# Attention and mixture-of-experts layer on one core: output weights pair by pair, logits in the attention's bank, router work half a step later

## What is computed

```python
# attention: 16 heads of size 64
n = layernorm(x)
q, k, v = (einsum('bsd,hde->bhse', n, W) for W in (Wq, Wk, Wv))
p = softmax(causal(q @ k.T / sqrt(64)))
y = n + concat_heads(p @ v) @ Wo
x = x + layernorm(gamma * norm(y, eps=1e-3) + beta)
# mixture of 8 experts, 2 for each token
t = layernorm(x)
probs = softmax(t @ router_w)              # the "logits" are t @ router_w
top_p, top_i = top_k(probs, 2)
out = sum over the 2 experts: top_p * (gelu(t @ w1[e]) @ w2[e])
x = x + layernorm(out)
```

## Time before and how to read the profile

| | us |
|---|---|
| median of 3 runs | 779.05 |
| lowest and highest | 778.43, 781.7 |
| profiled execution, its own time | 777.79 |
| its span, first to last instruction | 776.0 |
| PE busy | 720.2 (93%) |
| PE weight loads busy | 603.3 (78%) |
| DVE busy | 580.1 (75%) |
| ACT busy | 521.5 (67%) |
| POOL busy | 290.2 (37%) |

### The profile page before, as it was taken

How to read it: one execution, slowest core, us unless ns; L and a number is a source line. 1 busy time by engine, 2 the same in 40 slices (tenths; PEclk the granted TensorE clock), 3 DMA queues, 4 the chain that set the end, 5 groups by cost and what they waited for, 6 DMA issues and landing times.

```text
span 776.0 us, 17672 instructions
## 1 busy us (share of the span) xinstructions
PE 720.2 (93%) x5954; PEld 603.3 (78%) x5955; DVE 580.1 (75%) x1914; ACT 521.5 (67%) x1687; POOL 290.2 (37%) x404
## 2 busy tenths in 40 slices
PE   4999999999999999999999999999977789999954
PEld 3788878878788788878888888878767779999921
DVE  4668898989888888988889888988877444444316
ACT  4777777878777777877777777877754434444506
POOL 3024444232333423242333423241416555555525
PEclk9999999999999999999999999999979999999978
DMA  8620000000000000000000000000021132222145
GB/s 180 198 40 8 8 15 16 14 23 8 22 12 18 22 16 20 11 22 8 22 12 19 22 15 22 9 15 8 16 64 49 56 116 81 70 77 72 49 156 187
DMA packets 43701, 34.88 MB, mean 45 GB/s; under 512 B 10624, under 2 KB 40320, under 8 KB 43616
## 3 DMA queue, kind: packets, MB, share of 16 engines
q1 hardware_dynamic: 37984, 23.81, 11.4%
q0 software_dynamic: 4544, 9.45, 3.4%
q10 hardware_dynamic: 1088, 0.54, 0.2%
HBM read 20.22 MB, written 13.56 MB: 44 GB/s over the span
## 4 chain that ended last, share of the span: by engine, by line
PE 83%; DVE 4%; issue 4%; ACT 3%; POOL 2%; another core or an unknown queue 1%; DMA 1%; DVEq 1%; POOLq 0%; ACTq 0%; SPq 0%
PE PT1O L421 11%; PE M L383 9%; PE SC L404 8%; PE A L432 7%; PE A L664 7%; PE M L385 6%; PE M L384 6%; PE SC L412 4%; PE PT1O L441 4%; PE PT L446 3%; PE PT L445 3%; PE SC L407 3%; PE SC L383 2%; PE SC L385 2%; POOL expert_rows L1465 2%
## 5 line engine op out<-in xcount | busy, mean ns | idle before, releaser
L1201 ACT ACTIVATE qk<-M 128x512 f32<-128x512 f32 x127 | 76.0, 599 | 104.6 <-PE M L385 102.9
L1212 ACT ACTIVATE prob<-SC,nmax 128x256 f32<-128x256 f32 x256 | 125.4, 490 | 0.0
L1465 POOL DMA_INDIRECT expert_rows<-v_sb,got x78 | 77.4, 993 | 61.8 <-issue 31.1
L421 PE MATMUL PT1O<-pT,v_sb 128*64 128x256 f32 (+1 forms) x1024 | 98.6, 335 | 0.7 <-ACT pT L1217 0.7
L1206 ACT ACTIVATE prob<-SC,nmax 128x128 f32<-128x128 f32 x256 | 96.4, 377 | 4.3 <-DVE nmax L767 4.3
L421 PEld LDWEIGHTS PT1O<-pT,v_sb 128*64 128x64 f32 x1024 | 64.1, 138 | 42.7 <-ACT pT L1217 23.4
L775 DVE TENSOR_TENSOR prob<-prob,rden 128x512 f32<-128x512 f32 x128 | 92.5, 723 | 4.5 <-DVE rden L773 0.2
L1457 POOL DMA_INDIRECT sent_rows<-rec,slot x64 | 69.8, 1090 | 55.0 <-DVE slot L975 37.2
L767 DVE TENSOR_REDUCE nmax<-SC 128x2 f32<-128x512 f32 x128 | 87.1, 680 | 0.0
L383 PE MATMUL M<-xt_hi,wqk_hi 128*128 128x256 f32 x254 | 82.3, 324 | 4.4 <-ACT xt_st L1196 1.4
L664 PE MATMUL A<-w_sb,hidT 128*128 x624 | 78.0, 279 | 6.7 <-ACT v_sb L1335 3.3
(11 more groups left out here) (193 smaller groups left out, 1821.9 us busy)
## 6 DMA issues: line engine op xcount, KB each, us to landing
got<-sent_rows SPq DMA_DIRECT2D x39, 132.0 KB
w_in<-expert_rows SPq DMA_DIRECT2D x16, 256.0 KB, 3.5
x_in<-L_attn_x SPq DMA_DIRECT2D x16, 128.0 KB, 2.0
w_in<-L_ffn_w SPq DMA_DIRECT2D x1, 2048.0 KB, 12.1
x_res<-L_attn_x SPq DMA_DIRECT2D x16, 128.0 KB, 2.0
w_sb<-L_ffn_w SPq DMA_DIRECT2D x8, 256.0 KB, 4.7
out<-y_out SPq DMA_DIRECT2D x8, 256.0 KB, 2.1
sent_rows<-pad_rec SPq DMA_DIRECT2D x11, 132.0 KB, 4.8
```

What stands on the lines that cost most here:

```text
L421: last = mm(PT1O[k * E:(k + 1) * E, cols], v_sb[:, t, h * E:(h + 1) * E], src[:, par, k, :], start=(t == 0), stop=(t == 1), skip_group_che ...
L1212: return a.activation(prob[:, slot, k, 1:3, :].rearrange("p n t -> p (n t)"), SC[par][:, k, LATE_Q], ACT.Exp, bias=nmax[:, par, 0, k:k + 1 ...
L1465: q.indirect_dma_start(back, bass.IndirectOffsetOnAxis(ap=got[:, k, t, C_ID:C_ID + 1].bitcast(I32), axis=0), yo[:, k, t, :], None).then_in ...
```

## The change

- `w_o(c)` multiplies one pair's output weights (four matmuls in place of eight). A step calls it twice: where it stood, for the first of the two pairs, and behind the second transposes, for the other.
- PE's count of tokens (u = 0) and the logits (u = 1) move behind that second call. The logits are written to a free part of bank A instead of M; in exchange DVE's `attended`, which reads A, waits for them, and the next batch's first output weights wait until DVE has read them.
- On DVE router stage 3 moves behind `attended` in u = 1, stage 4 from the end of u = 1 into u = 2, stage 5 from u = 2 into u = 3, stage 6 from the middle of u = 3 to its end.
- On ACT the pT0 copies and the second Q/K copy each move ahead of one exponential, the copy of x ahead of `exps_late(p, 0)`, and `router_exp` to the end of u = 1. The last exponential of pair p, which signals `exp_done`, now stands behind the second pT0 copy.

The diff, cut to its core:

```diff
+        def logits_out(attending):
+            return A[:, T * D + (T + 1) * NE:T * D + (2 * T + 1) * NE] if attending else M[:, 0:T * NE]
...
             def w_o(c):
-                for par in range(2):
-                    for t in range(T):
-                        last = mm(A[:, t * D:(t + 1) * D], hT[:, par, t * P:(t + 1) * P], wo_sb[:, c + par, :],
-                                  start=(c == 0 and par == 0 and t == 0), stop=(c + par == NP - 1),
-                                  skip_group_check=True)
-                if c == NP - 2:
+                par = c % 2
+                for t in range(T):
+                    last = mm(A[:, t * D:(t + 1) * D], hT[:, par, t * P:(t + 1) * P], wo_sb[:, c, :],
+                              start=(c == 0 and t == 0), stop=(c == NP - 1), skip_group_check=True)
+                if c == NP - 1:
                     last.then_inc(sem("wo_mm"), 1)
...
-            def logits(r):
+            def logits(r, dst, fresh):
                 pe.wait_ge(sem("xfT_sb"), r + 1)
                 for t in range(T):
-                    last = mm(M[:, t * NE:(t + 1) * NE], xfT[:, t * P:(t + 1) * P], rw_sb[:],
-                              start=(t == 0), stop=True, skip_group_check=True)
+                    last = mm(dst[:, t * NE:(t + 1) * NE], xfT[:, t * P:(t + 1) * P], rw_sb[:],
+                              start=(fresh and t == 0), stop=True, skip_group_check=True)
...
# TensorE, step
-                if u == 0 and there(b, 3):
-                    rows_before(b - 3, before_out(True), False)
-                if u == 1 and there(b, 2):
-                    if more:
-                        pe.wait_ge(qk_sb, p + 3)
-                    logits(b - 2)
...
                 if k >= 2:
                     pe.wait_ge(o_sb, k - 1)
                     if u == 2 and there(b, 1):
                         pe.wait_ge(sem("att_done"), b)
+                        if there(b, 2):
+                            pe.wait_ge(sem("lg_done"), b - 1)
                     if u == 1 and there(b, 3):
                         pe.wait_ge(sem("before_sb"), b - 2)
                     w_o((c - 4) % NP)
...
-                    if u == 1 and there(b, 2):
-                        pe.wait_ge(sem("lg_done"), b - 1)
...
                     p_transpose(p - 1)
+                if k >= 2:
+                    w_o((c - 3) % NP)
+                if u == 0 and there(b, 3):
+                    rows_before(b - 3, before_out(True), False)
+                if u == 1 and there(b, 2):
+                    logits(b - 2, logits_out(True), False)
...
# VectorE, step
                     normalise_pair(p - 1)
-                if u == 1 and there(b, 2):
-                    router(b - 2, 3)
                 maxima(p + 1)
...
-                if u == 1 and there(b, 1):
-                    attended(b - 1)
+                if u == 1:
+                    if there(b, 1):
+                        attended(b - 1)
+                    if there(b, 2):
+                        router(b - 2, 3)
                 if u == 2:
                     if there(b, 1):
                         first_norm(b - 1)
                     if there(b, 2):
-                        router(b - 2, 5)
+                        router(b - 2, 4)
                 if u == 3:
                     if there(b, 1):
                         finish(b - 1)
                     if there(b, 2):
-                        router(b - 2, 6)
+                        router(b - 2, 5)
...
                     if there(b, 1):
                         attention_stats(b - 1)
-                    if there(b, 2):
-                        router(b - 2, 4)
...
-                if u == 3 and there(b, -2):
-                    x_stats(b + 2)
+                if u == 3:
+                    if there(b, -2):
+                        x_stats(b + 2)
+                    if there(b, 2):
+                        router(b - 2, 6)
...
             def attended(b):
                 dve.wait_ge(sem("wo_mm"), b + 1)
+                if there(b, 1) and there(b, -1):
+                    dve.wait_ge(sem("logit_mm"), b)
...
# ScalarE, step
                 exps_early(p, 0)
-                exps_late(p, 0)
...
                     xt_copy(b + 1)
+                exps_late(p, 0)
                 if k >= 1:
                     pT0_copy(p - 2)
-                if u == 1 and there(b, 2):
-                    router_exp(b - 2)
-                exps_late(p, 1)
                 if more:
                     qk_copy(p + 3)
-                exps_early(p, 1).then_inc(exp_done, 1)
+                exps_late(p, 1)
                 if k >= 1:
                     pT0_copy(p - 1)
+                exps_early(p, 1).then_inc(exp_done, 1)
...
                 if k >= 1:
                     o_copy(k)
+                if u == 1 and there(b, 2):
+                    router_exp(b - 2)
```

More of the change, by code:

```diff
@@ L592, in closing @@
                     w_o(NP - 4)
+                    w_o(NP - 3)
                     rows_before(B - 3, before_out(True), False)
@@ L600, in closing @@
                     w_o(NP - 2)
+                    w_o(NP - 1)
                 if j == 2:
@@ L603, in closing @@
                 if j == 3:
-                    logits(b - 2)
+                    logits(b - 2, logits_out(False), True)
                 if j == 6:
@@ L927, in router @@
                 if j == 3:
-                    logits = M[:, 0:T * NE].rearrange("p (t e) -> p t e", t=T)
+                    logits = logits_out(there(r + 2)).rearrange("p (t e) -> p t e", t=T)
                     dve.wait_ge(sem("logit_mm"), r + 1)
```

## The result

The changed kernel takes 775.08 us (median of 7 runs, 773.47 to 776.0) against 779.36 (7 runs, 778.43 to 782.38) for the kernel before: a ratio of 0.9931, with a 95% interval of 0.991 to 0.9952. It is faster by 0.7%; I had forecast 1.35%. The profiled execution took 774.88 us, its span 773.1, against a forecast of 767.2 for it.

The account below looks back on a forecast made before the run. PE's list was taken to bound the attention. A full batch summed to -0.79 us, 13 batches to 10.3, in all -10.6: profiled 767.2, median 768.5 us; range from 764.5 less half a microsecond to 776.5.

Parts of the forecast that it names:

- u = 0: Attention step with token counts, first transposes (X) to probabilities times V (R): claimed +0.03 us, counts costing the same.
- u = 1: Attention step with the logits, first transposes (X) to probabilities times V (R): claimed 4.51 us against 5.04, -0.53.
- u = 2: Attention step with x's transposes, first transposes (X) to probabilities times V (R): claimed 4.39 us against 4.57, -0.18.
- u = 3: Attention step with nothing extra on PE: claimed +0.12 us, 0.03 as a plain step and 0.09 for a late DVE.
- first two batches: Batches 1 and 2 of 16: claimed to have only the transposes' part of the gain, 0.2 us in all.
- idle load ahead of u = 3: PE's weight load waiting for DVE's split of the next batch's x: claimed to go, -0.23 us a batch.
- Unwaited, V to R is 0.80: From V product (V) to probabilities times V (R): claimed 0.80 us without waits, using the 0.23 pitch between V matmuls.
- wait (b): Ahead of probabilities times V (R): claimed 0.10 us of waiting for the pT0 copy, which the split would remove.
- The wait at Y: Second transposes (Y): claimed a new 0.37 us wait for DVE's normalisation, 2.19 us after the first transposes (X).
- My rival of a shorter last hop: Chain ahead of second transposes (Y) 0.1 us shorter in u = 0, 1 and 3: about 764.5 us, chance 0.12.
- my rival came true once: DVE pays in u = 3: GpSimd holds up the added router work, PE waits in u = 0; about 779, chance 0.22.
- The clock's rival: Tail after 560 us: more time at the lower clock level, up to 17 us back, 785 us; chance 0.06.

Follow-up runs that it names:

- Experiment 10: Changed kernel with only ScalarE's copy of pT0 for pair p - 2 moved ahead of one exponential: 771.18 us, 0.9891 of the kernel before.
- experiment 2: Kernel before with only the output weights split and the token counts behind the second group: 772.76 us, 1.0103 of the kernel before.
- experiment 6: Changed kernel with DVE's normalisation of pair p - 1 ahead of its copy for pair p - 2: 759.76 us, 0.9938 of the kernel before.
- experiment 8: Changed kernel with the logits, still in bank A, moved ahead of the second Q/K product: 756.1 us, 0.9884 of the kernel before.
- experiment 4: Changed kernel with router stages 4, 5 and 6 back in their old slots: 763.14 us, 0.9996 of the kernel before.
- experiment 5: Changed kernel run again unaltered, beside the next three runs: 759.67 us, 0.9927 of the kernel before.
- experiment 3: Changed kernel with ScalarE's old order of exponentials and copies, the router's exponential staying at the end of u = 1: 758.48 us, 0.9924 of the kernel before.
- experiment 1: Changed kernel with both pairs' output weights back in one group ahead of the second Q/K product: 748.91 us, 0.9788 of the kernel before.
- experiment 7: Changed kernel with three output-weight products ahead of the second Q/K product, one behind the second transposes (u = 2 all ahead): 747.92 us, 0.9787 of the kernel before.
- experiment 9: Changed kernel with both DVE's normalisation ahead of its copy and ScalarE's pT0 copy ahead of one exponential: 769.75 us, 0.9871 of the kernel before.

## Why the prediction came out at half

The direction was right and the range held the time; the size was off. That the range held it owes something to luck: the two largest misses, u = 2 and the first two batches, were in none of my rivals. The gain of a batch was 0.33 instead of 0.79, by the forecast's terms:

| term | forecast | measured |
|---|---|---|
| u = 0 | +0.03 | +0.11 |
| u = 1 | -0.53 | -0.49 |
| u = 2 | -0.18 | +0.17 |
| u = 3 | +0.12 | +0.10 |
| idle load ahead of u = 3 | -0.23 | -0.22 |
| first two batches, together | -0.2 | +1.7 |
| last batch and tail | -0.1 | -0.5 |

The rows of u = 0 to u = 3 are those of a usual batch; the late step of the third batch (0.66 us) and the one u = 2 of 5.01 (0.27) come on top. Thirteen batches miss 10.3 - 4.1 = 6.2 us, the first two 1.9, and the end gives 0.4 back: the 7.7 by which the profiled execution missed (774.88 against 767.2).

- **The step that failed: u = 2's term of the sum**, "1.77 + 0.80 + 1.02 + 0.80 = 4.39". Measured: 1.94 + 0.88 + 1.05 + 0.87 = 4.74, 0.35 a batch, three quarters of the miss. Two parts of it were mis-sized and one waiter was left out. The copy of x starts 0.11 later than X + 1.28 and T 0.06 later still. I costed ScalarE's reordering at nothing since "V and R have 0.445 us more PE work ahead of them". But the transposes at Y wait for the pT0 copy too (`pt0_sb, p - 1` stands right ahead of them in the code), and nothing was put ahead of Y. Experiment 10 moves that copy and gets 0.13 back. The rest is V to R (0.87 for 0.80), next, and 0.03 from Y to V.
- **"Unwaited, V to R is 0.80"** was never reached: in all steps of the full batches, of every kernel, it is 0.86 or more. The 0.80 had R start 0.23 behind V's third matmul, the pitch of two V matmuls, and put the other 0.10 down to the pT0 copy. But R comes 0.33 behind the third matmul before (322.15, 322.48) and 0.32 after (321.58, 321.90), although the pT0 copy ends 0.11 ahead of R before and 0.44 ahead after, at 321.46:

```profile
320.86 0.60 ACT L1228 ACTIVATE pT<-PT 128x512 f32<-128x512 f32 x1
```

  So wait (b), the second that the split was to remove, did not exist. The 0.03 by which V to R did shrink (0.90 to 0.87) lies between V's first and second matmul: 0.34 where V had waited for bank M, 0.32 where not. That makes the split a loss in plain steps: experiment 2 shows it alone (+0.11 in u = 0, +0.16 in u = 3, +0.15 in u = 1 and 2). I had called it even.
- **The wait at Y: size right, owner wrong.** 2.19 came true in u = 0, 1 and 3. DVE's normalisation is not what sets it (experiment 6), ScalarE's copy is (experiment 10), with DVE's chain 0.15 shorter. In u = 3 of the changed kernel the normalisation ends at 319.79 and the copy at 319.88, and Y is at 319.98:

```profile
319.28 0.60 ACT L1228 ACTIVATE pT<-PT 128x512 f32<-128x512 f32 x1
```

  The row of Y names DVE all the same. I took the owner from the row of k = 1, which names DVE too. My rival of a shorter last hop was not seen.
- **u = 0** lost 0.08 more: it is a plain step (+0.10, as in u = 3) with the counts moved at their own cost.
- **u = 3** is right by luck. The 0.09 for a late DVE did not come (X to Y 2.18); V to R (0.07 over its 0.80) and Y to V (0.03 over) stand in its place.
- **u = 1** was right, 4.55 against 4.51. But the gain came from the logits' bank, not from their place: placed ahead of the Q/K product in the same bank they reach 4.19 (experiment 8), and with the same place and the split but in bank M they take 5.19 (experiment 2). No run moved the bank alone.
- **The router slots** were right in mechanism: the idle load goes with them. Without them (experiment 4) the time is that of the kernel before, and the thirteen full batches take 3.5 of the 4.1 us back. DVE's work fitted in u = 3 in twelve of these batches. In the third batch it did not, and my rival came true once, with stage 5 taking the 1.8 us that I had named as a sign. The clock's rival did not come.
- **The start-up** cost 1.7 us where I had a gain of 0.2, the step of the sum that failed next in size (1.9 us of the 7.7); I had only looked at full batches. Up to the second o_copy it is chance: 38.92 here but 38.09 in experiment 5, the same kernel, against 38.05 for the kernel before. From the second to the eighth o_copy these two profiles take 50.24 and 50.20 us against 49.43. That 0.8 is the plain steps' loss by the split: experiment 2, the split alone, takes 50.24 too. ScalarE's order has no share that shows (50.20 in experiment 3).

Of the change's parts, then: the bank for the logits and the router slots win, the split loses most of that (0.87 of the 1.20 us a batch that experiment 1 has against the kernel before), the reordering is neutral. Leaving the split out (experiment 1) gives 2.1% in place of 0.7%; the uneven split of experiment 7 gives the same.

## What to carry to other kernels

Before splitting a group of matmuls to fill a wait, list every semaphore that stands at the point which loses its cover, and for each the end of the work behind it. The profile names one releaser only. Here the two chains differed by 0.15 us: shortening the earlier one gave nothing (experiment 6), the later one alone 0.15 (experiment 10), both 0.28 in u = 0 (experiment 9). Work that fills a wait belongs ahead of that wait, up to the length of the slowest chain there. A little more than that cost nothing here: all four products ahead and three of four give 33.60 and 33.56 a batch (experiments 1 and 7). An "unwaited" interval is safe only if some step of the trace shows it: one worked out from a neighbouring pitch should be entered with the shown one as a bound.

## What the hardware showed that I had not expected

- From the V product's last 128x512 matmul to the first product with the probabilities PE takes 0.31 to 0.34 us, not the 0.23 between two of the V matmuls: in every full batch of the kernel before, and in the changed kernel. Both copies of the transposed probabilities had ended 0.44 us or more before (u = 3 of the changed kernel). Where the pT0 copy ends only 0.05 ahead of R, it is 0.38 (experiment 1). What the 0.33 consists of was not tried.
- How soon PE starts behind the copy of ScalarE that it waited for depends on the place: 0.05 us at V (copy of Q/K ending at 321.53, V 321.58 in the kernel before), 0.10 at Y (319.88 and 319.98), 0.14 at T in u = 2 (310.72 and 310.86). Behind DVE's normalisation it is 0.05 at Y (358.67 and 358.72). So a releaser that ended 0.1 us ahead by its row can be the right one or the wrong one. What decides the difference was not tried.
- The kernel before took 763.5, 764.65 and 779.15 us on three chips. The changed kernel's two profiles have spans of 773.1 and 756.1 us; 15.7 of these 17.0 us lie behind the last o_copy. A change of 0.7% can only be read against the kernel before on the same chip.
